# Second stage reordered: one run of gram per tile, and the second half of the last pair of lookups in one block

## The reference

```python
e = jnp.stack([tbl_0[ids[:, 0]], ..., tbl_25[ids[:, 25]]], axis=1)
all_emb = jnp.concatenate([bottom_output[:, None, :], embeddings], axis=1)
gram = jnp.einsum('bfd,bgd->bfg', all_emb, all_emb)
z = gram[:, _TRIU_I, _TRIU_J]
h = jnp.concatenate([z, r_bottom_output], axis=1)
h = jnp.maximum(h @ W_top1 + b_top1, 0.0)
h = jnp.maximum(h @ W_top2 + b_top2, 0.0)
y = h @ W_top3
```

## Time and profile before

| | |
|---|---|
| Runs | 103.47, 102.46, 103.40 us; median 103.4 |
| Span of the profiled execution | 100.5 us |
| Own time of the profiled execution | not given; the median of the runs is 2.9 us above its span |
| Granted TensorE clock, mean | 1.000 |
| Busy: PE, PE weight loads, DVE, ACT, POOL | 95.8, 83.0, 66.4, 58.1, 60.6 us |

### The profile page before, as it was taken

One profiled execution on the slowest core, in us unless ns is written; L12 is line 12 of the kernel. 1 busy time (PEld: TensorE's weight loads), 2 busy tenths in 40 slices (PEclk: granted clock), 3 DMA queues, 4 the chain that ended last, 5 costly groups with the idle time before them and its releaser, 6 DMA issues.

```text
span 100.5 us, 3571 instructions
## 1 busy us (share of the span) xinstructions
PE 95.8 (95%) x1512; PEld 83.0 (83%) x1512; DVE 66.4 (66%) x164; ACT 58.1 (58%) x97; POOL 60.6 (60%) x64
## 2 busy tenths in 40 slices
PE   3999999999999999999999998999999999899992
PEld 3798687888888888888979987889989989798980
DVE  2499999999999999989797009206630681078001
ACT  5556959958996999994945304352433345312341
POOL 2678777787787787777777777777777700000000
DMA  2999979999999999999982221222222200000000
GB/s 46 265 267 263 198 222 243 227 224 232 217 193 216 231 233 232 221 219 245 252 249 85 52 59 52 59 59 52 59 59 52 62 26 7 0 7 0 1 7 0
DMA packets 6544, 13.55 MB, mean 135 GB/s; under 512 B 2076, under 2 KB 2860, under 8 KB 6528
## 3 DMA queue, kind: packets, MB, share of 16 engines
q1 hardware_dynamic: 4536, 9.51, 40.6%
q0 software_dynamic: 1824, 3.74, 15.6%
q10 hardware_dynamic: 168, 0.07, 0.3%
HBM read 13.30 MB, written 0.01 MB: 132 GB/s over the span
## 4 chain that ended last, share of the span: by engine, by line
PE 86%; DMA 5%; ACT 3%; SPq 2%; issue 1%; ACTq 0%
PE acc L663 34%; PE acc L729 12%; PE acc L763 12%; PE acc L691 8%; PE ring L703 6%; PE ring L774 5%; DMA raw<-tbl 5%; PE acc L754 4%; SPq L299 2%; PE ring L737 1%; PE ring L787 1%; ACT hi L376 1%; PE ring L798 1%; ACT onehot L420 1%; ACT emb L461 1%
## 5 line engine op out<-in xcount | busy, mean ns | idle before, releaser
L359 POOL DMA_INDIRECT rows<-tbl,ids_sb x57 | 59.9, 1050 | 18.7 <-issue 17.1
L547 DVE TENSOR_SCALAR onehot<-far 125x512 fp32r<-125x512 f32 (+2 forms) x92 | 32.2, 408 | 1.6 <-ACT far L390 1.6
L663 PE MATMUL acc<-onehot,hi 125*128 125x512 f32 (+1 forms) x84 | 23.8, 406 | 0.2 <-ACT onehot L420 0.2
L663 PE MATMUL acc<-onehot,lo 125*128 125x512 f32 (+1 forms) x84 | 22.3, 390 | 0.0
L663 PEld LDWEIGHTS acc<-onehot,lo 125*128 125x128 f32 x84 | 16.1, 193 | 3.0
L663 PEld LDWEIGHTS acc<-onehot,hi 125*128 125x128 f32 x84 | 15.5, 195 | 3.7 <-DVE onehot L547 0.6
L533 DVE TENSOR_TENSOR lo<-raw,hi 125x512 fp32r<-125x512 f32 (+1 forms) x24 | 16.8, 701 | 0.6 <-ACT hi L376 0.5
L568 DVE COPY gram<-acc 128x432 f32<-128x432 f32 x4 | 3.7, 915 | 19.8 <-PE acc L729 19.8
L376 ACT CAST hi<-raw 125x1024 fp32r<-125x1024 f32 (+1 forms) x11 | 12.0, 1090 | 7.0 <-DMA raw<-tbl 2.9
L729 PE MATMUL acc<-emb 128*27 128x27 f32 x1024 | 12.6, 193 | 0.9 <-ACT emb L461 0.4
L729 PEld LDWEIGHTS acc<-emb 128*27 128x27 f32 x1024 | 10.7, 104 | 3.4 <-issue 1.4
(11 more groups left out here) (53 smaller groups left out, 84.2 us busy)
## 6 DMA issues: line engine op xcount, KB each, us to landing
raw<-tbl SPq DMA_DIRECT2D x9, 448.0 KB
raw<-tbl SPq DMA_DIRECT2D x2, 560.0 KB
ids_b<-ids SPq DMA_DIRECT2D x4, 256.0 KB, 10.5
rows<-tbl,ids_sb POOLq DMA_INDIRECT x57, 8.3
w1z<-w SPq DMA_DIRECT2D x3, 234.0 KB
w_sb<-w SPq DMA_DIRECT2D x1, 512.0 KB
raw<-tbl SPq DMA_DIRECT2D x9, 52.0 KB
raw<-tbl SPq DMA_DIRECT2D x2, 224.0 KB
```

Of the source, the lines that this page charges most:

```text
L359: nc.gpsimd.indirect_dma_start(out=rows[:, t, slot, :], out_offset=None, in_=tables[table], in_offset=bass.IndirectOffsetOnAxis(ap=ids_sb[ ...
L547: ins = nc.vector.tensor_scalar(onehot[:, n % OH_RING, k, of], far[:, t % FAR_RING, of], float(c), None, ALU.is_equal)
L663: mm = nc.tensor.matmul(acc[:, look_bank(t), 0:looked_up(t)], part_of[:, t % HL_RING, c * D:(c + 1) * D], onehot[:, n % OH_RING, k, 0:look ...
```

## The change

The part of `ORDER` behind the last full lookup is written anew. Each gram is one step of all 32 groups. The four half lookups of the second 256 samples stand in one block behind the first gram, where pieces of gram stood between them. The other steps are placed around that: `bottom`, `turn`, `pairs`, `l1` and `l2` change places among each other and against the grams. The code that handled pieces of a gram goes. Waits are the same kind for each step, but the two shared banks follow the new order, so the use that each step waits for can be another. Nothing is added to the work or taken from it, and POOL's and SP's streams stay.

```diff
-    order += [
-              ("part", NL - 2, 0), ("part", NL - 2, 1), ("part", NL - 1, 0), ("part", NL - 1, 1), ("turn", 1, 2),
-              ("gram", 0, (0, 8)), ("bottom", 0, 0), ("turn", 1, 3), ("turn", 2, 0), ("part", NL - 2, 2),
...
-              ("pairs", 3, 0), ("bottom", 3, 1), ("columns", 0, 0), ("l1", 3, 0), ("l1", 3, 1), ("l1", 3, 2),
-              ("l1", 3, 3), ("l2", 3, 0), ("l2", 3, 1), ("l3", 3, 0)]
+    order += [("part", NL - 2, 0), ("part", NL - 2, 1), ("part", NL - 1, 0), ("part", NL - 1, 1), ("turn", 1, 2),
+              ("bottom", 0, 0), ("turn", 1, 3), ("gram", 0), ("turn", 2, 0), ("part", NL - 2, 2), ("part", NL - 2, 3),
+              ("part", NL - 1, 2), ("part", NL - 1, 3), ("pairs", 0), ("bottom", 0, 1), ("gram", 1), ("turn", 2, 1),
...
+              ("l1", 3, 2), ("l1", 3, 3), ("l2", 3, 0), ("l2", 3, 1), ("l3", 3)]
+    order = [step if len(step) == 3 else (*step, 0) for step in order]
...
-                    start, end = part
-                    if start == 0:
-                        if t == 0:
-                            pe.wait_ge(emb_bot, 1)
-
-                        pe.wait_ge(emb_part, t + 2 if t < TILES // PARTS else 4)
-                        pe.wait_ge(emb_turned, turn_count(t, TURNS - 1))
-                    for k in range(start, end):
+                    if t == 0:
+                        pe.wait_ge(emb_bot, 1)
+
+                    pe.wait_ge(emb_part, t + 2 if t < TILES // PARTS else 4)
+                    pe.wait_ge(emb_turned, turn_count(t, TURNS - 1))
+                    for k in range(U):
```

More of the change, by code:

```diff
@@ L118, in work_order @@
     order.append(("compare", NL - 1, 0))
-    order += [
-              ("part", NL - 2, 0), ("part", NL - 2, 1), ("part", NL - 1, 0), ("part", NL - 1, 1), ("turn", 1, 2),
-              ("gram", 0, (0, 8)), ("bottom", 0, 0), ("turn", 1, 3), ("turn", 2, 0), ("part", NL - 2, 2),
-              ("gram", 0, (8, 20)), ("part", NL - 2, 3), ("part", NL - 1, 2), ("gram", 0, (20, 32)),
-              ("part", NL - 1, 3), ("turn", 2, 1), ("gram", 1, (0, 4)), ("bottom", 0, 1), ("gram", 1, (4, 12)),
-              ("turn", 2, 2), ("pairs", 0, 0), ("gram", 1, (12, 16)), ("bottom", 1, 0), ("l1", 0, 0), ("turn", 2, 3),
[3 rows of a table removed]
-              ("turn", 3, 3), ("bottom", 2, 0), ("pairs", 2, 0), ("gram", 3, (0, 20)), ("bottom", 2, 1), ("l1", 2, 0),
[3 rows of a table removed]
+    order += [("part", NL - 2, 0), ("part", NL - 2, 1), ("part", NL - 1, 0), ("part", NL - 1, 1), ("turn", 1, 2),
+              ("bottom", 0, 0), ("turn", 1, 3), ("gram", 0), ("turn", 2, 0), ("part", NL - 2, 2), ("part", NL - 2, 3),
+              ("part", NL - 1, 2), ("part", NL - 1, 3), ("pairs", 0), ("bottom", 0, 1), ("gram", 1), ("turn", 2, 1),
+              ("l1", 0, 0), ("l1", 0, 1), ("turn", 2, 2), ("l1", 0, 2), ("l1", 0, 3), ("turn", 2, 3), ("pairs", 1),
+              ("bottom", 1, 0), ("l2", 0), ("gram", 2), ("bottom", 1, 1), ("l1", 1, 0), ("l1", 1, 1), ("turn", 3, 0),
+              ("l1", 1, 2), ("l1", 1, 3), ("pairs", 2), ("turn", 3, 1), ("l2", 1), ("bottom", 2, 0), ("bottom", 2, 1),
+              ("l1", 2, 0), ("l1", 2, 1), ("turn", 3, 2), ("turn", 3, 3), ("bottom", 3, 0), ("gram", 3), ("l1", 2, 2),
+              ("l1", 2, 3), ("l2", 2), ("pairs", 3), ("bottom", 3, 1), ("l1", 3, 0), ("l1", 3, 1), ("columns", 0),
+              ("l1", 3, 2), ("l1", 3, 3), ("l2", 3, 0), ("l2", 3, 1), ("l3", 3)]
+    order = [step if len(step) == 3 else (*step, 0) for step in order]
     return order
@@ L472, in _ @@
                 elif step == "gram":
-                    if not part[0] < UNIT <= part[1]:
-                        continue
                     if t >= 2:
@@ L562, in _ @@
                 elif step == "gram":
-                    if part[1] != U:
-                        continue
                     if t >= 2:
```

## The result

| | before | changed | ratio, 95% interval |
|---|---|---|---|
| Median of the runs, us | 102.93 | 115.42 | 1.1205 (1.1107 to 1.1303) |
| Lowest and highest, us | 102.03, 103.47 | 115.06, 118.9 | |
| Span of the profiled execution, us | 100.5 | 113.8 | |
| Granted TensorE clock, mean | 1.000 | 0.955 | |

The changed kernel is 12% slower. Forecast were 103.3 us and a range up to 105.5. The profiled execution of the changed kernel took 115.58 us around its span of 113.8, so 1.8 us lie around a span (the prediction's 2.9 set one execution's span against the median of all), and the 13.3 us between the two spans are the change's. A kernel here has executions some per cent slower than its others; the ratios leave these out, the medians do not.

The account below looks back on a forecast made before the run. PE in its own order was taken as the bound. Boundaries -2.3, waits for ACT and DVE +1.15 and instruction supply +1.1 summed to -0.05 us: 103.3 us, range 101.8 to 105.5.

Parts of the forecast that it names:

- Part 1, boundaries: Second stage on PE: gram in 4 blocks instead of 12 saves 0.29 us a block, -2.3 us.
- ways in and out: Steps next to a gram block: 0.09 us extra going in, 0.10 coming out, per block.
- The ramp: Inside each gram block: a fixed cost of 0.10 us per block, saved for eight blocks.
- The line of 0.07 + 0.00875 per record: Gram block time in us, fitted through blocks of 32 and 160 records; the source of the ramp.
- Part 2, waits for ACT and DVE: PE handovers in the new order: 1.95 us of new waits against 0.8 old, +1.15 us.
- Part 3, the supply of instructions: In three of four grams PE waits 0.38 us for an instruction packet, +1.1 us.
- then slower: Sign for late instructions: a hole of 0.7 us or more standing in each gram.
- The upper bound, 3.6 us in all: Most that late instruction packets could cost: four grams at 0.9 us each.
- I put nothing down to the clock: Granted PE clock: stays at 1.00, as the change leaves no gap of microseconds on PE; no cost.
- The slower one: Rival: each gram stands still once for 0.8 us, +3.2 instead of +1.1, time 105.4; chance 0.25.
- Its threshold of 0.7 us a gram: Wait per gram from which the rival of late instructions decides, the sum passing +1.0 us (104.4).

Follow-up runs that it names:

- cut_two: Changed kernel with each gram cut into two halves of 256 PE instructions, slow steps between them; 107.08 us, ratio 1.0380 to the kernel before.
- rest_new: Kernel before up to turn (2,1), then the new order with grams 1, 2 and 3 in one run each; 114.05 us, ratio 1.1079.
- spread: Three other orders of the kernel before's steps, with 8, 11 and 9 blocks of gram, chosen with a small model; 104.46, 105.16 and 105.80 us.
- filled: Changed kernel with two dead 128 by 512 matmuls in the middle of each gram, 8 in all; 111.72 us.
- stream_small: Kernel before plus 512 more gram-sized matmuls in one stream behind the last step; 127.48 us, the stream taking 26 us.
- stream_wide: Kernel before plus 128 matmuls of 128 by 128 in one stream behind the last step; 129.93 us.
- first_new: Kernel before with the new order only up to turn (2,1), so gram 0 in one run; 105.56 us, ratio 1.0255.

## Why the prediction was wrong

- **Part 1, boundaries.** The boundary prices were partly right: with four blocks PE's timeline has four ways in and out. The ramp did not come out as a gain: from start to end, less the holes, the four grams take 3.61, 3.59, 2.97 and 2.49 us, 12.7 in all. The twelve blocks before, read in the same way, took 12.0 (12.3 with their hole of 0.30), and eight ramps of 0.10 less would have been 11.2. The line of 0.07 + 0.00875 per record went through the two fastest blocks: the 64 at 77.69 took 0.89 us until 78.58, where it gives 0.63, and the 128 at 66.57 took 1.71, where it gives 1.19. In the changed kernel the 128 at 55.39 took 1.82 at a clock of 1.00, those at 79.78 1.28. What slows a block from inside stays open.
- **Part 2, waits for ACT and DVE.** Right. The handovers forecast at 1.95 us can be read in the timeline as the step between two starts over the step's own price: layer 2 of tile 0 0.14 and tile 1 0.48, gram 3 0.57 (the row at 97.12, marked "issue" but by its place the wait for the copies of the last turns), pairs 3 0.44, layer 1 of tile 3 0.34, gram 1 0.12: 2.1 us.
- **Part 3, the supply of instructions, is the step that failed.** The mechanism was named, and mis-sized by a factor of eight: +1.1 us forecast, and the holes at the six packets are 1.16, 1.63, 1.58, 0.47, 2.17 and 1.99, together 9.0 us. Each gram has one of 1.58 us or more, which is the sign that the prediction named for "then slower". Two things in "the transfer 1.0, plus a request ... (I take 0.5, the middle), minus 1.12: 0.38" were wrong. The time from one packet to the next is 3.45 us, not 1.5: behind the landing lie another 1.4 us until PE runs on, and 1.0 or more until the next transfer begins. So PE stands still for some 3.45 - 1.12 = 2.3 us a packet of gram, and for 2.38 and 2.72 us where `cut_two` and `rest_new` had their longest. And it was counted for the second packet of a gram only, three times, where six packets had a hole. The upper bound, 3.6 us in all, had the same fault: it let the unseen part be no longer than the transfer.
- **The row that said it.** The earlier trace rows has two packets 3.9 us apart, and I read that as plenty of room. Five stretches of the second stage of before, of which three are shown, PE alone (weight loads come on top, 120 to 141 in each):

```profile
59.70:63.50 3.80, 3.39 (x118) 1.00 0.22 56
...
67.20:70.90 3.70, 3.64 (x141) 1.00 0.22 55
...
74.70:78.40 3.70, 3.70 (x138) 1.00 0.21 57
```

  238 to 282 instructions in each 3.7 or 3.8 us: the old order already used PE's instructions at close to one packet per 3.45 us, evenly. That its cuts in the grams made it even is my reading; `cut_two` and the `spread` orders show that cuts alone do not. An average of 256 per 3.9 us next to a hole of 0.30 was a limit nearly reached.
- **"I put nothing down to the clock"** failed with it. Behind the holes of gram 0 and gram 2 the clock stood at its lower level. Against the same steps at full clock: the turn at 59.45 0.28 more, the lookup rows at 60.22 and 61.23 0.78, the bottom step at 83.48 0.47, layer 1 at 84.50 and 87.91 1.22 and 0.69, the turn at 87.06 0.41: 3.9 us. `filled`, with the clock at 1.000, shows these steps at their old prices.
- **The sum as measured**: holes 9.0 for 0.3 before, clock 3.9, handovers 2.1 for 0.8, longer grams +0.7 (12.7 for 12.0), and 0.1 that turn (1,2) began later (51.85 for 51.76): +14.7. With ways in and out at the forecast's -1.5, which the rows of all twelve blocks were not read for, 13.2 of the 13.3 us.
- **Rivals.** The slower one was the right one in kind (instructions late in each gram), with 3.2 us as its price and a chance of 0.25. Its threshold of 0.7 us a gram fits three grams; with four, -2.3 + 1.15 passes +1.0 at 0.54. Of the Trainium skill's two statements in "Advanced Engine Details and Errata", section "ISA Cache", the trace bears out the one on two lines of 256 instructions. The period alone would not, since one request at a time gives it with any number of lines; but the stream stands still after 438 instructions, behind slow steps that left time to fetch more, where the eight lines that 128 KB would be had room for 2048 (an estimate from that section's 256 a line).

## What to carry to other kernels

Count PE's instructions per time as well as its busy time: here PE can be given 256 of them per 3.45 us at best, 13.5 ns each, so a matmul with its weight load costs 27 ns of supply however small it is, and runs faster (8.75 ns a record) only while the packets at hand last, 219 records at the start of the stream. Put runs of tiny matmuls between steps of few, long ones, and see a cut that looks like waste as pacing until the packets of the instruction queue are far apart. When a range rests on a part of a delay that no row shows, the part seen is no bound for it.

## What the runs showed of the hardware that I had not expected

- PE goes on with a packet of its instructions only 1.1 to 1.4 us after the transfer has ended (1.4 in `stream_small`), and the next transfer begins 1.0 us behind that, or not until PE has used up a packet's worth (14 to 15 us in `stream_wide`). The shortest period is 3.45 us with all other DMA queues idle or with gathers running, and with the clock at either level; in `rest_new` two starts in gram 2 lay 4.01 us apart (78.77 to 82.78).
- What takes the clock to 0.50 is not settled. It fell behind holes of 1.16 and 1.63 us with 128 records between them, behind 0.47 and 2.17, behind a single 2.38 in `cut_two`, and in `rest_new` behind the handover of 2.35 and the hole of 2.35. It did not behind single holes of 1.15 (`first_new`), 1.58 and 1.99, nor behind 0.17 and 2.72 in `rest_new`. In the changed kernel PE's work at the lower level cost 40% as much again as the holes did.
- Adding 7.7 us of dead matmuls made the changed kernel 3.2% faster.
